# Two passes of a graph network that gather each edge tile once, with copies on VectorE and an identity product on TensorE

## What is computed

```
# layer 0
neigh_sum = segment_sum(h[src], dst);  deg = segment_sum(1, dst)
x = x + (neigh_sum / (deg + EPS)) @ W.T + b
# layer 1
eh = relu(concat([h[src], h[dst]]) @ W_edge.T)
x = x + relu((segment_sum(eh, dst) / max(cnt, 1)) @ W_node.T + b_node)
```

## Time and profile before

| | us |
|---|---|
| median of 3 runs | 6826.46 (6823.77 to 6831.67) |
| the profiled execution's own time | 6823.64 |
| its span | 6821.9 |
| busy: PE, PE weight loads | 3345.8, 2897.9 |
| busy: DVE, ACT, GpSimd (POOL) | 2697.0, 2103.5, 3437.8 |
| chain that ended last: share of an unnamed releaser | 48% |
| mean granted TensorE clock | 0.636 |

### The profile page before, as it was taken

How to read it: one execution, slowest core, us unless ns; L and a number is a source line. 1 busy time by engine, 2 the same in 40 slices (tenths; PEclk the granted TensorE clock), 3 DMA queues, 4 the chain that set the end, 5 groups by cost and what they waited for, 6 DMA issues and landing times.

```text
span 6821.9 us, 113042 instructions
## 1 busy us (share of the span) xinstructions
PE 3345.8 (49%) x30004; PEld 2897.9 (42%) x30005; DVE 2697.0 (40%) x6412; ACT 2103.5 (31%) x6369; POOL 3437.8 (50%) x3641
## 2 busy tenths in 40 slices
PE   1545445444444454454454534444444555555555
PEld 1434334333333343444444534444444455555454
DVE  4222223211111144444444544444445644444445
ACT  1111112222222233444444434444444322222222
POOL 3666664455555525555555355455454444444443
PEclk9565666767776665556555655555666666666666
DMA  4222222222222222222222232222222333333332
GB/s 114 91 87 88 90 85 83 80 74 78 75 76 77 75 56 75 78 78 82 78 78 82 56 83 81 77 78 81 77 77 62 103 97 100 96 98 96 98 95 80
DMA packets 342830, 564.68 MB, mean 83 GB/s; under 512 B 90413, under 2 KB 160957, under 8 KB 342622
## 3 DMA queue, kind: packets, MB, share of 16 engines
q0 software_dynamic: 124288, 289.37, 16.1%
q1 hardware_dynamic: 218354, 273.42, 12.7%
HBM read 490.31 MB, written 72.84 MB: 83 GB/s over the span
## 4 chain that ended last, share of the span: by engine, by line
another core or an unknown queue 48%; DVE 17%; PE 14%; issue 13%; ACT 3%; DVEq 2%; ACTq 1%; POOL 1%; DMA 0%; SPq 0%; POOLq 0%
PE psA L1564 7%; PE psDS L1189 3%; DVE acc L1683 2%; PE psDS L1542 2%; DVE prod L1589 1%; PE psA L1230 1%; DVE lg L1598 1%; DVE seg L1605 1%; DVE lastmax L1615 1%; DVE lastmax L1613 1%; DVE below L1661 1%; DVE V L1670 1%; DVE prod L1396 1%; DVE lastmax L1617 1%
## 5 line engine op out<-in xcount | busy, mean ns | idle before, releaser
L1165 POOL DMA_INDIRECT GT<-table,srcI x3520 | 3355.5, 953 | 3202.6 <-DVE V L1670 1403.7
L1564 PE MATMUL psA<-V,O 128*128 128x144 f32 (+1 forms) x4176 | 988.6, 425 | 10.8 <-ACT psA L1500 5.5
L1189 PE MATMUL psDS<-nodeQ,Ot 128*128 x2816 | 605.7, 390 | 658.3 <-ACT Ot L1181 559.8
L1564 PEld LDWEIGHTS psA<-V,O 128*128 128x128 f32 x4176 | 918.0, 314 | 17.2 <-issue 11.8
L1189 PEld LDWEIGHTS psDS<-nodeQ,Ot 128*128 128x128 f32 x2816 | 544.6, 290 | 696.4 <-issue 691.3
L1519 PE MATMUL psDS<-stageD,Ot 128*128 128x16 bf16 x4224 | 251.4, 173 | 804.2 <-issue 802.9
L1519 PEld LDWEIGHTS psDS<-stageD,Ot 128*128 128x128 bf16 x4224 | 184.3, 102 | 878.2 <-issue 860.4
L1683 DVE TENSOR_TENSOR acc<-acc,psA 128x1296 f32 (+1 forms) x261 | 381.2, 1460 | 413.8 <-remote 349.8
L1661 DVE TENSOR_TENSOR below<-lg,psDS 128x128 f32<-128x128 f32 (+1 forms) x264 | 62.4, 236 | 1157.8 <-remote 1156.6
L1500 ACT COPY psA<-consts 128x1296 f32<-128x1296 f32 (+1 forms) x261 | 315.0, 1207 | 628.4 <-DVE acc L1683 471.9
L1550 PE MATMUL psDS<-newM,Ot 128*128 128x16 bf16 (+1 forms) x6336 | 256.5, 175 | 430.2 <-issue 291.3
(11 more groups left out here) (244 smaller groups left out, 5286.0 us busy)
## 6 DMA issues: line engine op xcount, KB each, us to landing
Ob<-onehots SPq DMA_DIRECT2D x352, 256.0 KB
Ot<-onehots_turned SPq DMA_DIRECT2D x352, 256.0 KB
GT<-table,srcI POOLq DMA_INDIRECT x3520
onehots<-Ob SPq DMA_DIRECT2D x88, 256.0 KB
onehots_turned<-Ot SPq DMA_DIRECT2D x88, 256.0 KB
first<-first_dram SPq DMA_DIRECT2D x176, 64.0 KB
first_dram<-GT SPq DMA_DIRECT2D x18, 384.0 KB, 5.1
table<-nodeQ SPq DMA_DIRECT2D x40, 128.0 KB, 1.9
```

Of the source, the lines that this page charges most:

```text
L1165: eng.indirect_dma_start(out=GT[:, p.k, j, 0:table.shape[1]], out_offset=None, in_=table, in_offset=bass.IndirectOffsetOnAxis(ap=srcI[:, p ...
L1189: ins = eng.matmul(psD[:, j, :], Ot32[:, p.q, j, :], at_block(nodeQ, b[j], D), start=True, stop=True)
L1564: ins = eng.matmul(to, O[:, p.q, j, :], V[:, p.q, j, 0:VW], start=False, stop=j == G - 1, skip_group_check=True)
```

## The change

**Gathers by tile.** In the sum pass and the MLP pass, GpSimd gathers each of the 665 tiles once, in 84 groups of eight tiles, the last with one (`fetch_tiles`, written out without a loop). It reads the indices from `srcT` itself, which now holds them by tile. The rows land in a ring of 32 tiles in a new buffer, `rows_of_edges`. Before tile group n GpSimd waits for `over` of the step group that used tile group n - 4 last; the number of that step group is loaded from `tiles_over` into a register. After the fifth gather of group n it waits until group n - 1 has landed and raises `landed`. The order by steps, which the GAT and dot passes still need, is stored to HBM in the setup (`src_steps`) and loaded into `srcT` by SP near the end of the MLP pass.

**A reader of the ring** takes eight slot numbers and two values of `landed` from tables (`landed_steps`), with one wait for each half of the eight steps.

**Sum pass.** DVE copies the rows of each step from the ring to the place from which PE multiplies them, eight copies a group behind the addition of group p - 1, and signals `copied`. PE waits for `copied` instead of the gathers, and `copied` frees the ring.

**MLP pass.** PE adds the rows itself: behind each product with `nodeQ` stands one of the identity with the step's rows, into the same PSUM place. ACT applies ReLU to PSUM. DVE's addition (`prod`) and ACT's index copies are gone. `toedge`, PE's signal, frees the ring.

**Setup.** Three more loads bring `src` by tile. DVE makes the tables of slots, landed groups and freeing groups, with seven operations more on one partition at the end. Some small tiles now lie in `Ot32`.

```diff
+        def fetch_tiles(eng, table, over):
+            tables_stored(eng)
+            to = by_tiles(table.shape[1])[1]
+            def has_landed(n):
+                eng.wait_ge(*ring_tiles[n % RING](n // RING, min(G, T - n * G) - 1))
+                eng.sem_inc(landed.sem, 1)
+            for n in range(NT):
+                k = n % RING
+                if n >= RING:
+                    eng.wait_ge(*over(loaded(eng, "over", tiles_over, n - RING, 1, NG - 1, for_waits=True)[0]))
+                    apart(eng)
+                for t in range(n * G, min(n * G + G, T)):
+                    eng.indirect_dma_start(
+                        out=to[:, t % (RING * G), :], out_offset=None, in_=table,
+                        in_offset=bass.IndirectOffsetOnAxis(ap=srcT[:, t:t + 1], axis=0),
+                    ).then_inc(ring_tiles[k].sem, 16)
+                    if t % G == G // 2 and n:
+                        has_landed(n - 1)
...
+        def landed_steps(eng, p, of):
+            ring = by_tiles(D)[1]
+            last = isinstance(p.g, int) and p.g == NG - 1
+            at = loaded(eng, "slots", slots_of_steps, p.g, G, RING * G - 1)
+            need = loaded(eng, "need", tiles_needed, p.g, 2, NT - 1, for_waits=True)
+            parts = [(0, G // 2, need[0]), (G // 2, G, need[1])]
...
+            for a, z, group in parts:
+                eng.wait_ge(*landed(group))
...
+                for j in range(a, z):
+                    ins = of(j, ring[:, bass.ds(at[j], 1), :].rearrange("p o w -> p (o w)"))
+            return ins
...
@@ sum_pass: POOL, ACT, DVE, PE
-                    fetch_groups(eng, NG, table, sums)
+                    fetch_tiles(eng, table, copied)
...
-                        if p.has(RING):
-                            copy_index(eng, p.plus(RING))
...
                         if p.has(-1):
                             add_group(eng, p.plus(-1), True)
+                        if p.has(0):
+                            eng.wait_ge(*sums(p.g - RING))
+                            landed_steps(eng, p, lambda j, rows: eng.tensor_copy(by_tiles(D)[0][:, p.k, j, :], rows)).then_inc(copied.sem, 1)
...
-                            eng.wait_ge(*ring_rows[p.k](p.i))
+                            eng.wait_ge(*copied(p.g))
...
-                                ins = sum_of_step(eng, place[j], GT[:, p.k, j, 0:D], O[:, p.q, j, :], j == G - 1)
+                                ins = sum_of_step(eng, place[j], by_tiles(D)[0][:, p.k, j, :], O[:, p.q, j, :], j == G - 1)
@@ mlp_pass: POOL, SP, ACT, DVE, PE
-                    fetch_groups(eng, NG, table, prodded)
+                    fetch_tiles(eng, table, toedge)
...
+                    eng.wait_ge(*landed(NT - 1))
+                    eng.dma_start(srcT[:, :], src_steps).then_inc(src_loaded, 16)
...
-                            eng.wait_ge(*prodded(a.g))
+                            eng.wait_ge(*toedge(a.g))
                             eng.wait_ge(*sums(a.g - 2))
-                            eng.activation(V[:, a.q, :, 0:D], prod[:, :, :], ACT.Relu).then_inc(values.sem, 1)
+                            eng.activation(V[:, a.q, :, 0:D], psD[:, :, :], ACT.Relu).then_inc(values.sem, 1)
...
-                            eng.tensor_tensor(prod[:, :, :], psD[:, :, :], GT[:, a.k, :, 0:D], ALU.add).then_inc(prodded.sem, 1)
...
-                            rows_to_edges(eng, a, loaded(eng, "blocks", blk, a.g, G, NB - 1))
+                            b = loaded(eng, "blocks", blk, a.g, G, NB - 1)
+                            eng.wait_ge(*turned32(a.g))
+                            eng.wait_ge(*values(a.g - 1))
+
+                            def both_rows(j, rows):
+                                eng.matmul(psD[:, j, :], Ot32[:, a.q, j, :], at_block(nodeQ, b[j], D), start=True, stop=False)
+                                return eng.matmul(psD[:, j, :], ident[:, :], rows, start=False, stop=True)
+                            landed_steps(eng, a, both_rows).then_inc(toedge.sem, 1)
```

More of the change, by code:

```diff
@@ L50, in has, with sweep @@
         return not isinstance(self.g, int) or 0 <= self.g + d < self.n
-def sweep(eng, n, turn, early=0, late=0):
+def sweep(eng, n, turn, early=0, late=0, tail=0):
     head = -(-late // RING) if late else 1
-    last = (n - early) // RING
+    last = (n - max(early, tail)) // RING
     for p in range(-early, head * RING):
@@ L187, in loaded @@
             eng.load(regs, table[0:1, bass.ds(g * (of or n), n)])
+            if for_waits:
+                if (eng.engine, which, "held") not in reg_sets:
+                    reg_sets[eng.engine, which, "held"] = [eng.alloc_register(f"{which}_held_{j}") for j in range(n)]
+                held = reg_sets[eng.engine, which, "held"]
+                for r, to in zip(regs, held):
+                    eng.reg_alu(to, r, 0, ALU.max)
+                regs = held
             return [eng.snap(r, min_val=0, max_val=most) for r in regs]
@@ L199, in program @@
         noted.per = G
-        ring_rows = [Count(sem(f"rows{r}"), 1, 16 * G) for r in range(RING)]
+        ring_tiles = [Count(sem(f"tiles{r}"), G, 16) for r in range(RING)]
+        landed, copied, src_loaded = Count(sem("landed")), Count(sem("copied")), sem("src_loaded")
         ring_hot = [Count(sem(f"hot{r}"), 1, 16) for r in range(RING)]
@@ L323, in program @@
         TILES, FRESH = 1, 2
-        SRC, SLOTS_, LAST = 1, 2, 3
+        TILE_SRC, SRC, SLOTS_, LAST = 1, 2, 3, 4
         dst_f, src_f, last_r, first_r = rows[2:6]
+        tile_f = rows[7]
+        firsts_of_tiles = work[0:1, 1024:1024 + NT - RING]
+        assert (NT - RING) * G + 1 <= T and 1 << (G.bit_length() - 1) == G and RING * G & (RING * G - 1) == 0
         with nc.Block() as block:
@@ L337, in do @@
                     count += 1
+                do(eng.tensor_copy, tile_f, tile_rows)
+                marks["tiles"] = count
                 eng.wait_ge(columns, 16)
@@ L370, in _ @@
                     do(eng.tensor_copy, WG[k][:, D:D + 2 * HEADS1], psS[:, 64 * k:64 * k + 2 * HEADS1])
+                eng.wait_ge(tables_turned, TILE_SRC)
+                do(eng.tensor_copy, srcT[:, :], psN[:, 0:SC, :].rearrange("p c s -> p (c s)"))
+                marks["tiles out"] = count
                 eng.wait_ge(fetched, 16 * 2 * SC)
@@ L464, in _ @@
                 ins.then_inc(weights_turned, 1)
+                eng.wait_ge(prepared, marks["w1 w2"])
+                turn(tile_f)
+                eng.wait_ge(prepared, marks["tiles out"])
                 eng.wait_ge(prepared, marks["src"])
@@ L493, in program @@
         turned_hots = Ot32[:, :, :, :].rearrange("p q g e -> p (q g) e")
[L494 removed]
+        own_sums = [acc[:, u * H:(u + 1) * H, 0:D] for u in range(UNITS)]
         usual = Home([Ys[:, s, :] for s in slots], [YTs[:, s, :] for s in slots], banks, banks)
@@ L1346, in _ @@
                     rest_of_units(eng, phase, phase.tensor)
-            close((index, onehot, turned, onehotT, onehot32, sums, counted, added), NG)
-            rows_closed(NG)
+            close((onehot, turned, onehotT, onehot32, sums, counted, copied, added), NG)
+            tiles_closed()
+            hots_closed()
             phase.over()
@@ L1389, in turn @@
                             add_group(eng, p.plus(-1), False)
-                        begin_units(eng, phase, phase.vector, p, 0)
-                        if p.has(1):
-                            a = p.plus(1)
-                            eng.wait_ge(*ring_rows[a.k](a.i))
-                            eng.wait_ge(*toedge(a.g))
-                            eng.wait_ge(*values(a.g - 1))
-                            eng.tensor_tensor(prod[:, :, :], psD[:, :, :], GT[:, a.k, :, 0:D], ALU.add).then_inc(prodded.sem, 1)
-                        begin_units(eng, phase, phase.vector, p, 1)
-                    sweep(eng, NG, turn, early=1, late=1)
+                        for half in range(2):
+                            begin_units(eng, phase, phase.vector, p, half)
+                    sweep(eng, NG, turn, late=1, tail=1)
                     rest_of_units(eng, phase, phase.vector)
@@ L1419, in _ @@
                     rest_of_units(eng, phase, phase.tensor)
-            close((index, onehot32, turned32, toedge, prodded, values, sums, added), NG)
-            rows_closed(NG)
+            close((onehot32, turned32, toedge, values, sums, added), NG)
+            tiles_closed()
+            hots_closed()
             phase.over()
@@ L1817, in _ @@
                     phase.vector(eng)
-            close((index, onehot32, toedge, prodded, logit, logitT, segmax, segT, flagged, lastmaxed,
+            index.close(NG)
+            close((onehot32, toedge, prodded, logit, logitT, segmax, segT, flagged, lastmaxed,
                    lastmax1ed, lastmax2ed, nmax, pens, tmaxed, resets, carried, forward, newMed, newM1ed, newM2ed, drop, rescale,
```

(4 more changed lines are left out.)

112 lines of the change are left out of this document (77 added, 35 removed).

## The result

| | before | changed |
|---|---|---|
| median | 6826.46 us (6819.57 to 6838.56, 7 runs) | 6802.95 us (6791.52 to 6810.87, 7 runs) |
| ratio | | 0.9963, 95% interval 0.9951 to 0.9974 |
| span of the profiled execution | 6821.9 us | 6798.9 us |
| chain that ended last: part of the span that it could be followed through | all | from 2506.8 us on |
| unnamed releaser, share of that chain behind 2506 us | 39% | 39% |

The account below looks back on a forecast made before the run. GpSimd's gathers plus pauses ended by held TensorE updates were taken as the bound. Sum pass +109 (-49 + 158), MLP pass -192 (-49 - 143) and setup +4 gave -79 us, about 6747 us median; range 6560 to 6930 us.

Parts of the forecast that it names:

- What bounds the kernel: Sum and MLP passes: TensorE updates falling late in a gather burst are held until it ends; periods 23.7 and 28 us.
- Fewer gathers, -49 in each pass: Sum and MLP passes: 665 instead of 704 gathers, 39 x 1.255 = 49 us less in each, 98 in all.
- Sum pass, +158 for the later release: Sum pass: VectorE's copies free the ring, so the next gather starts 3.6 us later in each of 44 periods.
- S: The held TensorE update that arrives 2.9 us after a burst of gathers and that everything waits for.
- MLP pass, -143: MLP pass: `toedge` frees slots without product or index copy before the next gather; pauses fall from 320 to 177 us.
- The low clock: MLP pass: if TensorE's clock stayed low, its 48 records a group would cost 1 us a group, 88 us.
- Nothing between the passes: Stretches between passes: the forecast had no term for them; GAT and dot passes were put at 0.
- Setup +4: Setup: more loads, a second transposition, seven one-row operations and a store cost 4 us, bounds 2 and 10.
- the first: Rival, 20%: sum pass pauses do not grow because GpSimd may be a group further ahead; -237 us, 6590 us.
- Bursts of one group: Rival, 24%: in the sum pass updates are held after every eight gathers, 16.0 us a group; +115 us, 6940 us.
- Copies that stop gathers: Rival, 10%: each of 704 VectorE copies in the sum pass stops a gather for 0.228 us; +81 us, 6905 us.
- rival D: Follow-up rival, MLP pass: TensorE's chain sets a group's 12.2 us, so earlier register loads give -130 to -175 us.

Follow-up runs that it names:

- kernel with 704 gathers: The changed kernel with its ring filled by steps again, 704 gathers in 88 groups: 6880.47 us, ratio 1.0075 of the version before.

## Why the prediction came out as it did

*What bounds the kernel.* Right for the chip of the trace. The update that is held until a burst ends sets the rhythm of both versions there, and on free chips, with the same gathers and no held update, the version before is 1914 us faster. Wrong as a rule for the kernel: on five of the chips met the hold does not exist. The prediction never asked whether its rhythm belonged to the chip, and its one trace did not show it. That this did not spoil the forecast too is luck: the result was measured on a holding chip.

*Fewer gathers, -49 in each pass.* **This is the step that failed.** In the sum pass they came off. In the MLP pass GpSimd's rhythm goes by the 88 groups of steps, which the change leaves as they are, and the gathers saved came back as five pauses 9.6 us above the others: 48 of the 49 us that this term had counted. The kernel with 704 gathers shows it, 9 us longer in that pass for 39 gathers more. I had taken the release by `over` for a matter of one group each time, though the 39 steps without a tile of their own have to be waited for somewhere.

*Sum pass, +158 for the later release.* The mechanism was right: a pause of 7.2 us after 16 gathers, ended by the copies, 4.2 us behind S. The size was 20 us too high. The pauses, beyond the usual gaps of 0.3 us, rose from 156 to 291 us, by 136 and not 158: 41 pauses wait for copies, not 44, and one grew from 3.9 to 7.2 us, by 3.3 and not 3.6, because S came 2.9 us behind the last gather and not 3.2. Eight copies took 1.3 us, with 0.8 us of register loads ahead, together the 2.2 us that I had put down for copies alone. The pass grew by 88 us against 109.

*MLP pass, -143.* I took 177 us of pauses, about midway between passed and held (the middle of 153 and 206 is 179.5). Every update was held, the worse case, but each pause is 2.4 us of idle time, 2.1 beyond the usual 0.3, and all time beyond the usual gaps, added up over the pass, is 229 us. Without the five long pauses' 48 it would be 181, close to my figure by luck. TensorE's way behind S was 10.4 us, not 9. From the end of the cast to the first product it took 2.2 us, not 1.2: the two loads took the 1.1 us forecast (0.59 and 0.55), and the register operations and waits around them, which the sum had at nothing, took as much again. The low clock did not become the cover: the pass had a mean granted clock of 0.78, and TensorE was busy for 708 of 1065 us. The 88 us put down for that case did not follow from its own numbers either, 11.3 us of matmuls in a period of 12.

*Nothing between the passes.* Missed by 18 us. Behind the last gather of the MLP pass TensorE has three groups of products left (48 records of L1514 in the profile, against 32 of L1189 before), and that boundary grew by 12 us. The last group of tiles, which holds one tile, is not the reason: the kernel with 704 gathers has a full last group and still 51 such records behind its last gather, and 119.4 us there. Why TensorE is one group further behind stays open.

*Setup +4:* 4.4 us.

*The rivals.* The pauses of the sum pass did grow, so the first falls. Bursts of one group did not come: the sums that end on the third gather pass. They did come in the run freed by `sums`, and cost it a part of its gain. Copies that stop gathers did not show: 956 and 954 ns on the holding chip, 953 on the free one with the copies beside them. On the last, the Trainium skill (SBUF — State Buffer, "Who interferes with whom") lets copies and casts of VectorE in a two-port mode shut GpSimd out for the whole instruction. The trace agrees in part for the cast of 1024 elements: the gathers beside it get longer, but by 0.18 us on average and 0.52 at most, not by the 0.69 of the whole instruction. It shows nothing of it for the copies of 128 elements. Whether these ran in such a mode, no run shows; the measurement decides. The size of the miss, 55 us, is the five long pauses (48), the boundaries (18), 5 us in the later passes and 4 by which the other pauses of the MLP pass (181) passed my 177, less the 20 us by which the sum pass did better.

## What stays open

What holds the updates on one kind of chip is not known. Whether a gap in the gathers frees them, and whether TensorE's chain, started 2 us sooner, would get its update through, was expected in writing five times for each and met a holding chip in none. So rival D, that TensorE's chain and not the hold sets the 12.2 us of a group, was not tested by a run. The trace speaks against it: that chain needs 9.8 us with no gather beside it, and its products end 1.7 us before their update is seen. The best kernel seen on a holding chip is the changed one with its sum pass freed by `sums`, 6687.59 us, 1.7% below the changed kernel. On a free chip it was run only together with TensorE's moved waits, and has the changed kernel's ratio there, 0.9879.

## What to carry to other kernels

When a ring is freed by one kind of group and filled by another, count the groups that the freeing side still has to do: saved transfers come back as waits. Read what stands between the late signal and the first instruction that it releases, and move out of it whatever another engine's signal can stand for; here one word was worth five times the whole change. And before a rhythm is built into a prediction, know that it may belong to the chip on which the trace was taken.

## What the hardware showed that I had not expected

The same program takes 6826 us on some chips and 4910 on others, with gathers of 0.95 us and gaps of 0.30 on both. GpSimd's busy time is nearly the same too, 3438 and 3456 us, so for GpSimd the whole difference is idle time. The chain that ended last shows where it lies, version before, on a holding and on a free chip:

```profile
another core or an unknown queue 48%; DVE 17%; PE 14%; issue 13%; ACT 3%; DVEq 2%; ACTq 1%; POOL 1%; DMA 0%; SPq 0%; POOLq 0%
```

```profile
POOL 59%; issue 24%; DVE 6%; PE 4%; DMA 2%; ACT 2%; ACTq 1%; POOLq 1%; DVEq 0%; SPq 0%
```

A share of 48% for an unknown releaser in a kernel of one core was the sign: where updates arrive, GpSimd itself is the chain. Add up the shares of such a line before comparing two of them; a chain that is lost half-way looks like a gain. And a VectorE cast of 1024 elements to float32 slows the gathers beside it by 0.18 us on average and 0.52 at most, while copies of 128 elements do not slow them.
